# Two buffers of exponentials, a ring of eight blocks of expert weights, and a new set of moments for the planner

## The reference

```
xn = layernorm(x); x = x + attn0(xn) + moe0(xn)
xn = layernorm(x); x = x + attn1(xn) + moe1(xn)
```

## Time and profile before

| | |
|---|---|
| median of 3 runs | 686.4 us (685.87 to 688.39) |
| the profiled execution | 688.77 us |
| its span, first to last instruction | 686.2 us |
| TensorE matmul busy | 611.5 us (89%) |
| VectorE busy | 510.8 us (74%) |
| ScalarE busy | 436.5 us (64%) |
| GpSimd busy | 304.0 us (44%) |
| mean granted TensorE clock | 0.949 |

### The profile page before, as it was taken

One profiled execution on the slowest core, in us unless ns is written; L12 is line 12 of the kernel. 1 busy time (PEld: TensorE's weight loads), 2 busy tenths in 40 slices (PEclk: granted clock), 3 DMA queues, 4 the chain that ended last, 5 costly groups with the idle time before them and its releaser, 6 DMA issues.

```text
span 686.2 us, 12410 instructions
## 1 busy us (share of the span) xinstructions
PE 611.5 (89%) x3812; PEld 319.4 (47%) x3812; DVE 510.8 (74%) x1127; ACT 436.5 (64%) x811; POOL 304.0 (44%) x406
## 2 busy tenths in 40 slices
PE   2455698999999999989999999989999999999996
PEld 1322233555445454434654655547455465464521
DVE  4799979879778889976777587765767557657662
ACT  2413267787778778765667576655766567657685
POOL 3234882256756625754661215562563022121362
PEclk9876679999999999998999999999999999999999
DMA  8953324435466444456545354463654534433011
GB/s 242 287 158 108 105 64 158 133 108 169 143 169 175 120 146 138 133 162 202 147 138 158 107 160 142 130 178 117 183 161 138 162 91 142 132 113 121 25 51 36
DMA packets 83394, 95.25 MB, mean 139 GB/s; under 512 B 7554, under 2 KB 70530, under 8 KB 83330
## 3 DMA queue, kind: packets, MB, share of 16 engines
q1 hardware_dynamic: 79234, 86.08, 42.0%
q0 software_dynamic: 4096, 8.40, 4.4%
HBM read 67.84 MB, written 26.21 MB: 137 GB/s over the span
## 4 chain that ended last, share of the span: by engine, by line
PE 63%; DVE 16%; DMA 9%; SPq 5%; issue 4%; POOL 2%; ACT 2%; POOLq 0%; DVEq 0%; ACTq 0%
PE pv_ps L895 14%; PE slot L866 12%; PE slot L883 11%; PE slot L843 10%; PE slot L856 6%; DVE mx L1259 6%; DMA wbuf<-in_experts 4%; SPq L708 1%; PE slot L832 1%; PE slot L825 1%; PE slot L903 1%; DMA q_stack<-mxT 1%; PE slot L797 1%; DMA k_stack<-parts_hbm 1%; PE slot L875 1%
## 5 line engine op out<-in xcount | busy, mean ns | idle before, releaser
L1259 DVE TENSOR_REDUCE mx<-slot 128x1 f32<-128x512 f32 x512 | 331.0, 684 | 116.3 <-PE slot L866 114.1
L1015 ACT ACTIVATE probsT<-slot 128x512 f32<-128x512 f32 x512 | 281.7, 597 | 69.5 <-PE slot L883 68.0
L866 PE MATMUL slot<-k_stack,q_stack 72*128 72x512 bf16 x512 | 199.2, 396 | 20.9 <-DVE mx L1259 18.9
L883 PE MATMUL slot<-q_stack,k_stack 75*128 75x512 bf16 x512 | 191.5, 388 | 6.5 <-DMA q_stack<-mxT 3.5
L895 PE MATMUL pv_ps<-probsT,v 128*32 128x512 f32 x1024 | 139.6, 617 | 1.2 <-ACT probsT L1015 1.1
L1350 POOL TENSOR_TENSOR hid<-th,up 128x512 f32<-128x512 f32 (+2 forms) x56 | 71.0, 1269 | 129.1 <-DVE th L1122 64.2
L866 PEld LDWEIGHTS slot<-k_stack,q_stack 72*128 72x128 bf16 x512 | 50.3, 99 | 128.1 <-issue 51.7
L843 PEld LDWEIGHTS slot<-xgT,wbuf 128*128 128x128 f32 (+1 forms) x576 | 74.2, 187 | 29.1 <-issue 21.7
L843 PE MATMUL slot<-xgT,wbuf 128*128 128x128 f32 (+1 forms) x576 | 79.5, 282 | 6.8 <-DMA wbuf<-in_experts 6.8
L1338 POOL DMA_INDIRECT yg<-ys_hbm,index x64 | 61.7, 964 | 53.2 <-issue 35.5
L1327 POOL DMA_INDIRECT xs_hbm<-xn,index x64 | 64.3, 1005 | 42.2 <-DVE index L1249 25.9
(11 more groups left out here) (130 smaller groups left out, 576.0 us busy)
## 6 DMA issues: line engine op xcount, KB each, us to landing
wbuf<-in_experts SPq DMA_DIRECT2D x48, 544.0 KB, 4.6
q_stack<-parts_hbm SPq DMA_DIRECT2D x96, 96.0 KB
k_stack<-parts_hbm SPq DMA_DIRECT2D x96, 96.0 KB
wbuf<-in_experts SPq DMA_DIRECT2D x64, 128.0 KB, 2.6
xg<-xs_hbm SPq DMA_DIRECT2D x28, 256.0 KB, 3.5
ys_hbm<-ys SPq DMA_DIRECT2D x28, 256.0 KB, 4.2
parts_hbm<-parts SPq DMA_DIRECT2D x16, 384.0 KB, 4.1
xs_hbm<-zeros SPq DMA_DIRECT2D x2, 2048.0 KB, 12.6
```

Source lines behind the costliest of these rows:

```text
L866: nc.tensor.matmul(ps[:, 0:N], q_stack[0:STACK, h, j * P:(j + 1) * P], k_stack[0:STACK, h, :], start=True, stop=True).then_inc(slot_full, 1)
L883: nc.tensor.matmul(ps[:, 0:N], k_stack[0:STACK + MAXROWS, h, j * P:(j + 1) * P], q_stack[:, h, :], start=True, stop=True).then_inc(slot_fu ...
L1015: nc.scalar.activation(probsT[:, k % PROBS, a, :], ps[:, 0:N], ACT.Exp, scale=SCALE).then_inc(slot_free, 1)
L1259: nc.vector.tensor_reduce(mx[:, g, u // J, u % J:u % J + 1], ps[:, 0:N], AXIS.X, ALU.max)\
```

## The change

PROBS goes from 3 to 2 and layer 1's WBUF from 6 to 8. All moments in SETUP, ROUTE and GROUPS and the SLACK are other numbers. The planner's choice of a PSUM slot is now simply the lowest free one, where before a slot was preferred whose neighbour was in use; a slot still waits for the one use before it. The new constants MODE, SWITCH and STAY are empty or zero and have no effect. No instruction of the computation is added or removed.

```diff
-PROBS = 3
+PROBS = 2
-WBUF = (24, 6)
+WBUF = (24, 8)
...
-SETUP = (-10.64, -0.69, 2.73, 4.24, 9.02, 10.84, 14.41, 18.24)
-ROUTE = (0.51, 5.3, 12.26, 18.16)
-GROUPS = ((3.31, 0.51), (8.11, 0.64), (13.64, 1.12), (19.79, 1.59))
-SLACK = 0.4
+SETUP = (-0.028, -11.417, 1.535, 14.542, 12.34, 0.352, 14.703, 34.517)
+ROUTE = (-0.438, 22.318, 17.849, 28.987)
+GROUPS = ((0.947, 1.745), (19.829, 0.156), (21.218, 1.193), (27.556, 0.286))
+SLACK = 0.341
...
-        if WIDTH.get(kind, 1) == 1:
-            single = [k for k in free if k ^ 1 >= SLOTS or not vacant[k ^ 1]]
-            free = single or free
-        return free[0]
...
+                for fill in fills_of(stage):
+                    ring[fill] = vacant.index(True)
...
+            if plan.nth[stage]:
+                eng.wait_ge(free[plan.ring[stage]], plan.nth[stage])
```

More of the change, by code:

```diff
@@ L388, in engine_orders @@
     soon = {engine: [key for key in found if key[0] == engine and not missing[key]] for engine in ENGINES}
-    frees = {freer(stage): stage for engine, stage in found if engine == "PE" and stage[0] in FILLS}
+    frees = {freer(fill): fill for engine, stage in found if engine == "PE" for fill in fills_of(stage)}
     busy = {engine: 0.0 for engine in ENGINES}
@@ L393, in engine_orders, with room, change_of @@
     releases, times = [], []
[L394 to L402, removed]
-        if WIDTH.get(kind, 1) == 1:
-            single = [k for k in free if k ^ 1 >= SLOTS or not vacant[k ^ 1]]
-            free = single or free
-        return free[0]
+    now, left, close, mode = 0.0, len(found), 1e-9, 0
+    def room(stage):
+        fills = fills_of(stage)
+        return not fills or (sum(vacant) >= len(fills) and
+                             held[fills[0][0]] + len(fills) <= AT_ONCE.get(fills[0][0], SLOTS))
+    def change_of(key):
+        return STAY if key[0] == "PE" and MODE.get(key[1][0], 0) != mode else 0.0
     while left:
@@ L410, in engine_orders @@
             releases.remove(entry)
-            kind, k = entry[1][0], ring[entry[1]]
-            vacant[k:k + WIDTH.get(kind, 1)] = [True] * WIDTH.get(kind, 1)
-            held[kind] -= 1
+            vacant[ring[entry[1]]] = True
+            held[entry[1][0]] -= 1
         moved = False
@@ L417, in engine_orders @@
                 continue
[L418 to L421, removed]
+            could = [key for key in soon[engine] if open_at[key] <= now + close and (engine != "PE" or room(key[1]))]
             if not could:
                 continue
-            key = min(could, key=lambda k: (found[k].wanted, number[k]))
-            task = found[key]
+            key = min(could, key=lambda k: (found[k].wanted + change_of(k), number[k]))
+            task, stage = found[key], key[1]
             soon[engine].remove(key)
-            task.start, task.end = now, now + task.lasts
-            busy[engine] = now + task.holds
+            change = 0.0
+            if engine == "PE":
+                if MODE.get(stage[0], 0) != mode:
+                    change = SWITCH
+                mode = MODE.get(stage[0], 0)
+                for fill in fills_of(stage):
+                    ring[fill] = vacant.index(True)
+                    vacant[ring[fill]] = False
+                    held[fill[0]] += 1
+            task.start, task.end = now, now + change + task.lasts
+            busy[engine] = now + change + task.holds
             times += [busy[engine]]
-            orders[engine].append(key[1])
+            orders[engine].append(stage)
             left -= 1
             moved = True
[L433 to L437, removed]
             if key in frees:
@@ L453, in engine_orders, with fills_of @@
     return orders, ring, gated, found
+def fills_of(stage):
+    return [stage] if stage[0] in FILLS else []
 ENGINES = ("PE", "ACT", "DVE", "POOL", "SP", "IN")
-WIDTH = {}
+MODE = {}
+SWITCH = 0.0
+STAY = 0.0
 FILLS = set(FREED_BY)
@@ L469, in __init__ @@
         self.nth = {}
-        self.earlier = {}
         uses = [0] * SLOTS
-        latest = [None] * SLOTS
         for stage in self.orders["PE"]:
[L474 to L479, removed]
+            for fill in fills_of(stage):
+                self.nth[fill] = uses[self.ring[fill]]
+                uses[self.ring[fill]] += 1
     def before(self, a, b):
@@ L649, in vacant @@
         def vacant(eng, stage):
-            for old in sorted(plan.earlier[stage]):
-                eng.wait_ge(*emptied(old))
+            if plan.nth[stage]:
+                eng.wait_ge(free[plan.ring[stage]], plan.nth[stage])
         def tiles(A):
```

## The result

The changed kernel takes 696.25 us (median of 20 executions, 689.23 to 705.58) against 687.7 for the kernel before on the same chips (20 executions, 681.42 to 695.7). The ratio is 1.0123 with a 95% interval of 1.0096 to 1.015: slower by about 1.2%, clear of noise. The forecast was 678.0, so it missed the sign, and the time lies just above the range's upper end of 696. On the median before that the prediction started from, 686.4, the change costs 8.4 us (686.4 x 0.0123) where -8.2 was forecast; 16.6 us have to be explained.

What follows compares the result with a forecast made beforehand. TensorE was taken as the bound from 128.6 to 643 us, with reserve mostly at start and tail. Terms -6.8 - 2.9 + 0 + 1.5 = -8.2 from the 686.4 median gave 678 us; likeliest 672 to 683, range 664 to 696 (8 in 10).

Steps and rivals of the forecast that it cites:

- Middle: Layer 0's second route and eight groups become filler through layer 0 and the boundary: 0 us, bounds -3.3 and +3.3.
- the layer norm's 2.2 us: Sequence 3's layer norm, at 63.89 to 66.05, leaves the early stretch where VectorE is full: -2.2 us.
- Two buffers of exponentials: ScalarE's exponentials wait for products two chunks back instead of three; third buffer never needed: 0 us, bound above 1.5.
- Ring of eight: Layer 1's weight blocks no longer wait for the previous group's down matmuls: -6.8 us of TensorE waits, bounds 0 and -6.8.
- Start: First setup and the stretch where VectorE is full, new stage order: -2.9 us, bounds -5.0 and +2.9.
- Tail: Last group's down matmuls wanted 1.25 units later, mostly won back by the freed ring: +1.5 us, bounds -3 and +19.
- near 38: Sign at the end: us from the last DN's end to the span's end; more means the tail waits for gathers.
- The first rival: Setup at the layers' border makes VectorE and TensorE miss scores: slower, 696 us, chance 0.2.
- The second: Rival at the end: the tail keeps its 1.25 units' lateness, slower, 692 us, chance 0.07.
- The third: Rival: no change, the 6.8 us reopen as waits for VectorE or PSUM slots, 683 to 690 us, chance 0.16.
- the fourth: Rival: larger gain, groups no longer paced by the ring fill holes of middle and tail, 667 us, chance 0.19.
- in windows of several us around the change of layers: Sign at the layers' border: TensorE's idle growing there, or its granted clock falling, would prove the prediction wrong.

Runs made afterwards that it cites:

- after_yc_later: Changed kernel with only the combines YC(0,1) and YC(1,1) moved twelve places later in VectorE's list: 683.65 us, ratio 0.992 to the kernel before.
- after_pt_waits_mp_first: Changed kernel, GpSimd's parts of sequences 4 and 6 waiting for the two combines, one maxima stage (MP) put ahead of sequence 6's parts: 689.03 us, ratio 1.001.
- bufs_same_order: Kernel before with PROBS 2 and WBUF (24, 8) on the chip, planner still reckoning with the old sizes, so instruction order kept: 688.09 us, ratio 0.9978.
- bufs_replanned: Kernel before with only PROBS 2 and WBUF (24, 8), planned anew with old moments and old slot choice: 683.5 us, ratio 0.9911.
- before_yc_into_pt: Kernel before with YC(0,1) four places and YC(1,1) two places later on VectorE, beside GpSimd's parts: 703.54 us, ratio 1.0188.

## Why the prediction was wrong

**Where it failed.** It is the term "Middle: 0, bounds -3.3 and +3.3", which measured about +13.9 (the 2.0% between the changed kernel and after_yc_later; 1.1% of it, some 7.8 us, is shown with VectorE's order untouched, by after_pt_waits_mp_first). Under it lies the sentence that a sum of busy time is conserved in the middle and that moving a stage there changes nothing. That took the length of a VectorE stage for a constant. I costed the moved stages by their moments and never asked what GpSimd runs beside them. The hole of 3.3 us that the term spoke of is gone, but two others formed. The bounds were too narrow for a hole in any case: they hold the standstill alone, and not the low clock behind it, which the earlier trace rows show between 300 and 322 us (0.84). The sign was in a row that I had used: in the earlier trace rows a TENSOR_SCALAR on 128x4 takes 0.86 us, as long as four instructions on 128x128, and I added it into the layer norm's 2.2 us without asking why. The eight instructions of that line in the kernel before, with the shortest, the median and the longest in ns:

```profile
L1063 DVE TENSOR_SCALAR var_eps<-mv x8: 169/170/859, 8.8 to 399.6; 128x4 f32<-128x4 f32 x8
```

The normal length is 0.17 us. In the earlier trace rows it began at 65.19, inside a GpSimd instruction of the parts (64.88 to 66.03), and ended with it. That row, out of proportion to its size, was the warning that VectorE's work can take several times as long beside GpSimd. In the changed kernel the same line shows it once more, and the timeline names the neighbour:

```profile
64.14 1.15 POOL L1315 TENSOR_TENSOR rest<-qk,parts 128x512 f32<-128x512 f32 x1 [0.38 <-ACT parts L946]
64.20 1.11 DVE L1061 TENSOR_SCALAR var_eps<-mv 128x4 f32<-128x4 f32 x1
```

This instruction has one tensor operand, so it isn't only those with two that GpSimd holds up.

**Two buffers of exponentials, 0.** Right: no wait for pv_ps in bufs_same_order, and its ratio is not above 1.

**Ring of eight, -6.8.** Right in size: -6.1 by bufs_replanned (interval -3.6 to -8.6). In the changed kernel the step from DN to the next GG is 7.0 us, from 592.65 + 2.84 = 595.49 to 602.54 (timeline of TensorE),

```profile
592.65 2.84 PE L854 MATMUL slot<-wbuf,hid 128*128 128x128 f32 x24
...
602.54 0.72 PE L841 MATMUL slot<-xgT,wbuf 128*128 128x128 f32 x5
```

instead of 13.3, and 12 groups take 25.5 us each, (643.4 - 337.1) / 12, instead of 26.9. With the old order it measured only 0.2%, but that run had the second collision in it, so how much of the ring's gain needs the new plan stays open.

**Start, -2.9.** Right in size: TensorE's first E is at 83.10 us, before at 86.46, 3.4 earlier. Not by all of its parts, though: the first maximum is 1.6 us later (51.30 against 49.66, where my sign was 46 to 50), so the first setup lost and the stretch where VectorE is full gained more than I gave it.

**Tail, +1.5.** Harmless, as taken. The last DN ends at 640.68 + 2.68 = 643.36, 1.2 us earlier than before, so the later moment was won back by the ring:

```profile
640.68 2.68 PE slot L854 x24
```

(the chain that ended last, changed kernel). From there to the end of the span it is 43.3 us, before 41.6 (686.2 - 644.57), so the tail is 1.7 us longer, and attention ends it, not the experts: the last combine ends 4.45 us before attention's last addition starts (timeline of VectorE).

```profile
676.48 2.31 DVE L1156 SCALAR_TENSOR_TENSOR x<-yg,w_ab,x 128x128 f32<-128x128 f32 x8 [3.80 <-DMA yg<-ys_hbm,index]
...
683.24 0.69 DVE L1142 TENSOR_TENSOR x<-x,att 128x512 f32<-128x512 f32 x1
```

The "near 38" that I gave as a sign was worked out wrongly: even the kernel before has 41.6.

**The sum without the collision.** 0.992 is -5.5 us (interval -3.4 to -7.6) where -8.2 was forecast; 680.9 lies inside the 672 to 683 given for the likeliest case. It is also what the two sizes bring with the old moments (0.9911). So the moments and the slot choice bring nothing that these runs can tell.

**The rivals.** The first rival had the price, 696, one of the two places, the border of the layers (the other, at 238 us, is far from it), and the wrong mechanism. It decides if YC(0,0) comes less than 40 us before the scores need sequence 4. Layer norm 4 runs at 216.13 and the first maximum of sequence 4 after 359.89, so the reserve is 144 us, larger than before (136). That its number nearly fits is chance. The second fails with DN's end. The third and the fourth would both have shown a time under 690.

**The signs that I gave.** TensorE's idle growing "in windows of several us around the change of layers" and the clock falling there is what the profile shows at the second hole. That sign was right, and it was named as a symptom only; its cause in VectorE's row wasn't looked for. TensorE's idle was to fall to about 67 us; in the profiled execution, the fastest of the 20, it is 72.7 (686.7 - 614.0).

**What stays open.** Why making GpSimd wait ends at 1.001 and not at 0.992: its trace has the two standstills named above, untested. And why the changed kernel's executions spread over 16 us where those of after_yc_later spread over 10: its two traces differ in the third standstill at 497 us, which only the slower of them has.

## What to carry to other kernels

When stages are reordered, ask of each that lands elsewhere which GpSimd instructions run beside it, and not only what its own engine and its needs are doing: two operands in SBUF on VectorE beside a GpSimd tensor operation made 2.3 us into 5.9 here. Look in the profile of before for instructions that take much longer than others of the same line (median against longest), since they show which pairs disturb each other, and remember that such a wait is counted as busy. When several constants are changed together, time them in parts; here two of them hold all of the gain that these runs can tell, and the rest brings the loss.

## What was not expected of the hardware

One combine instruction of 0.346 us took up to 1.41 us, while GpSimd's of the same moments went from 1.16 to at most 1.31 us (L1315): the loss is nearly all on VectorE's side. The standstill of TensorE of 2.6 us in the changed kernel was followed by 6 us at a granted clock of 0.50, so that hole cost more after it had closed (some 3 us) than while it was open. That is no rule: in before_yc_into_pt a standstill of 2.64 us (473.2 to 475.8) was followed by 6 us at 1.00. What makes the difference these runs don't show.
